# Dividing the softmax at the attention output and exchanging one more unit of the long tiles

## What is computed

```python
x = x + layernorm(attention(layernorm(x)))     # 32 heads of 128 in 8 groups of 4, causal
x = x + layernorm(feed_forward(layernorm(x)))  # 512 -> 1792 -> 512, silu(gate) * up

qkv = q @ w_qkv.T                              # 4096 query, 1024 key, 1024 value columns
scores = einsum('bskgd,btkd->bkgst', qh, kh) / sqrt(128)
scores = where(causal, scores, min_float)
probs = softmax(scores, axis=-1)
attn = einsum('bkgst,btkd->bskgd', probs, vh)
return attn.reshape(...) @ w_dense.T
```

## Time and profile before

| | us |
|---|---|
| median of 3 runs | 1142.49 |
| lowest, highest | 1142.47, 1144.24 |
| span of the profiled execution | 1140.7 |
| TensorE busy in it | 1122.7 |
| VectorE busy | 833.9 |
| ScalarE busy | 626.1 |
| GpSimd busy | 713.9 |

### The profile page before, as it was taken

One profiled execution on the slowest core, in us unless ns is written; L12 is line 12 of the kernel. 1 busy time (PEld: TensorE's weight loads), 2 busy tenths in 40 slices (PEclk: granted clock), 3 DMA queues, 4 the chain that ended last, 5 costly groups with the idle time before them and its releaser, 6 DMA issues.

```text
span 1140.7 us, 17840 instructions
## 1 busy us (share of the span) xinstructions
PE 1122.7 (98%) x5512; PEld 945.5 (83%) x5512; DVE 833.9 (73%) x1987; ACT 626.1 (55%) x1350; POOL 713.9 (63%) x802
## 2 busy tenths in 40 slices
PE   8999999999999999999999999999999989999997
PEld 7888888888888888888888888888887768888885
DVE  5645454557888898888888888988579766666666
ACT  6532324237776767676767767776588532222224
POOL 7844447436674865856757748567784746665645
PEclk9999999999999999999999999999999999999999
DMA  6443555335466475485474665754410033333422
GB/s 224 138 158 148 184 203 185 148 128 183 129 194 218 152 224 183 142 265 173 143 262 127 206 205 159 240 172 121 167 65 1 20 115 114 109 111 92 121 65 98
DMA packets 154696, 173.76 MB, mean 152 GB/s; under 512 B 41776, under 2 KB 128496, under 8 KB 151280
## 3 DMA queue, kind: packets, MB, share of 16 engines
q1 hardware_dynamic: 154608, 172.68, 46.8%
HBM read 101.06 MB, written 71.57 MB: 151 GB/s over the span
## 4 chain that ended last, share of the span: by engine, by line
PE 93%; DVE 2%; POOL 2%; ACT 1%; issue 1%; DMA 0%; POOLq 0%; DVEq 0%; SPq 0%; ACTq 0%
PE psS L1813 29%; PE psOY L1942 17%; PE psOY L1957 15%; PE psOY L1813 15%; PE psT L1813 11%; PE psT L1920 5%; POOL x L1100 0%; DVE pT_lo L1468 0%; PE psS L1819 0%; POOL raw_up L1000 0%; DMA raw<-in_w_v 0%; DVE y L1612 0%; POOL rstd L1031 0%; POOL up_lo L896 0%; DVE probs_long L1533 0%
## 5 line engine op out<-in xcount | busy, mean ns | idle before, releaser
L955 POOL TENSOR_SCALAR probs_long<-probs_long,rsum 128x896 f32<-128x896 f32 (+9 forms) x124 | 129.0, 1042 | 62.3 <-DVE rsum L1539 60.9
L1269 ACT ACTIVATE probs_long<-probs_long,negmax 128x896 f32<-128x896 f32 (+9 forms) x124 | 121.4, 979 | 42.0 <-DVE negmax L1533 39.7
L955 POOL TENSOR_SCALAR probs_short<-probs_short,rsum 128x416 f32<-128x416 f32 (+15 forms) x128 | 69.0, 543 | 120.1 <-DVE rsum L1539 119.7
L1813 PE MATMUL psS<-kT_hi,qT_hi 128*128 128x256 f32 (+8 forms) x384 | 133.0, 346 | 0.0
L1813 PE MATMUL psS<-kT_hi,qT_lo 128*128 128x256 f32 (+8 forms) x384 | 128.3, 334 | 0.0
L1813 PE MATMUL psS<-kT_lo,qT_hi 128*128 128x256 f32 (+8 forms) x384 | 128.1, 334 | 0.0
L1957 PE MATMUL psOY<-wd_hi,oT_hi 128*128 128x512 f32 x256 | 106.8, 417 | 3.3 <-DVE oT_lo L1468 3.3
L1022 POOL TENSOR_SCALAR hidden<-mask,hr,hs 128x128 f32<-128x128 f32 x112 | 50.0, 456 | 86.2 <-DVE hr L1632 82.1
L1957 PE MATMUL psOY<-wd_hi,oT_lo 128*128 128x512 f32 x256 | 101.2, 395 | 0.0
L1957 PE MATMUL psOY<-wd_lo,oT_hi 128*128 128x512 f32 x256 | 100.5, 393 | 0.0
L1264 ACT CAST pT_hi<-square 128x1024 fp32r<-128x1024 f32 (+3 forms) x87 | 77.6, 892 | 31.6 <-DVE square L1552 31.2
(11 more groups left out here) (200 smaller groups left out, 3267.1 us busy)
## 6 DMA issues: line engine op xcount, KB each, us to landing
q_raw<-q_scr SPq DMA_DIRECT2D x64, 256.0 KB, 3.4
p_scr<-probs_long SPq DMA_DIRECT2D x24, 512.0 KB, 3.3
raw<-in_w_qk SPq DMA_DIRECT2D x10, 1024.0 KB, 5.6
p_scr<-probs_long SPq DMA_DIRECT2D x21, 448.0 KB, 2.5
probs_long<-p_scr SPq DMA_DIRECT2D x90, 96.0 KB, 2.8
q_scr<-cB SPq DMA_DIRECT2D x16, 512.0 KB, 2.6
q_scr<-cA SPq DMA_DIRECT2D x16, 512.0 KB, 2.7
raw_wd<-in_w_dense SPq DMA_DIRECT2D x8, 1024.0 KB, 8.4
```

The lines of the kernel that those rows point to most:

```text
L955: nc.gpsimd.tensor_scalar(row, row, rsum[:, column(t, h)], 1.0, ALU.mult, ALU.mult).then_inc(p_ready, 1)
L1269: nc.scalar.activation(row, row, ACT.Exp, bias=negmax[:, column(t, h)], scale=-1.0, accum_out=lsum[:, column(t, h)]).then_inc(e_done, 1)
L1813: last = nc.tensor.matmul(dst, a, b, start=(start and k == 0), stop=(stop and k == len(terms) - 1), skip_group_check=resumed)
```

## The change

1. All 27 exchanged tiles exchange all four units; units 3 and 2 have their low parts on GpSimd, units 1 and 0 on VectorE.

```diff
-    SWAPS = {4: (3, 2, 1), 5: (3, 2, 1), 6: (3, 2, 1), 7: (3, 2, 1, 0)}
-    POOL_LOW = {4: (), 5: (), 6: (), 7: (3,)}
+    SWAPS = {i: (3, 2, 1, 0) for i in range(TPB, NT)}
+    POOL_LOW = {i: (3, 2) for i in range(TPB, NT)}
```

```diff
+            def inverses_away(t):
+                sp.wait_ge(r_done, t + 1)
+                sp.dma_start(r_scr[t % INVERSES], rsum[:, t % INVERSES, :]).then_inc(r_out[t % INVERSES], 16)
+
+            def inverses_back(t):
+                sp.wait_ge(r_out[t % INVERSES], 16 * (t // INVERSES + 1))
+                if t >= 2:
+                    sp.wait_ge(o_scaled, t - 1)
+                sp.dma_start(inverses[t % 2][:], r_scr[t % INVERSES].rearrange("p u -> (p u)").unsqueeze(0).broadcast_to(
+                    [P, BANK])).then_inc(r_in[t % 2], 16)
...
-            def norm_head(t, h):
-                pool.wait_ge(r_done, softmax_count(t, h))
-                row = whole_row(t, h)[:, 0:keys_of(t, h)]
...
-                nc.gpsimd.tensor_scalar(row, row, rsum[:, column(t, h)], 1.0, ALU.mult, ALU.mult).then_inc(p_ready, 1)
+            def zero_tail(t, h):
+                pool.wait_ge(s_done, softmax_count(t, h))
+                nc.gpsimd.memset(probs_long[:, h, S - SPAN * (HG - 1 - h):S], 0.0).then_inc(tail_zero, 1)
+
+            def lo_of_output(t):
+                pool.wait_ge(o_hi, t + 1)
+                low(oT[1][:], o_sb[:], oT[0][:]).then_inc(o_done, 1)
...
-                    act.wait_ge(o_full, args[0] + 1)
-                    nc.scalar.copy(by_head(oT[0]), from_units(psO)).then_inc(o_hi, 1)
+                    act.wait_ge(o_scaled, args[0] + 1)
+                    if args[0] >= 1:
+                        act.wait_ge(y_full, args[0])
+                    nc.scalar.copy(oT[0][:], o_sb[:]).then_inc(o_hi, 1)
...
-            def inverse_sum(t, h):
-                dve.wait_ge(e_done, softmax_count(t, h))
-                nc.vector.reciprocal(rsum[:, column(t, h)], lsum[:, column(t, h)]).then_inc(r_done, 1)
+            def inverse_sums(t):
+                dve.wait_ge(e_done, LAST_SCORE[t] + 1)
+                if t >= INVERSES:
+                    dve.wait_ge(r_out[t % INVERSES], 16 * (t // INVERSES))
+                nc.vector.reciprocal(rsum[:, t % INVERSES, :], lsum[:, t % LANES, :]).then_inc(r_done, 1)
+
+            def scale_output(t):
+                dve.wait_ge(o_full, t + 1)
+                dve.wait_ge(r_in[t % 2], 16 * (t // 2 + 1))
+                if t >= 1:
+                    dve.wait_ge(o_done, t)
+                inverse = inverses[t % 2][:].rearrange("p (b q u) -> p b u q", b=HG, u=HG)
+                nc.vector.tensor_tensor(by_head(o_sb), from_units(psO), inverse, ALU.mult).then_inc(o_scaled, 1)
```

```diff
-                pe.wait_ge(p_ready, softmax_count(t, h))
+                pe.wait_ge(e_done, softmax_count(t, h))
...
-                        pe.wait_ge(o_done, t)
+                        pe.wait_ge(o_scaled, t)
...
+                elif t >= 1 and before_in_row(t) is not None:
+                    k = before_in_row(t)
+                    dve.wait_ge(t_full, TURN["P", k, p_banks(k) - 1, h] + 1)
```

4. New numbers in `PE_LATER`, `ACT_LATER`, `DVE_LATER` and `POOL_LATER` (the `..._MOVES` stay), and SP gets an order of its own for the attention part: a list `LOADS_IN_ORDER` of exchanges, inverses and loads, shifted by `SP_LATER`. Some of it:

```diff
-                ("PV", 0, 0): 2.3, ("X", 0): -37.5, ("DN", 1): -45.7, ("GU", 1): -37.7, ("S", 1, 0): -8.4,
+                ("P", 0, 0, 2): -87.4, ("P", 0, 0, 3): 18.2, ("PV", 0, 0): -12.9, ("PV", 0, 1): -14.8,
...
-            for t in range(2, T):
-                g, n = divmod(t, NT)
-                if t - 3 in SWAPPED:
...
+            for item in moved(LOADS_IN_ORDER, SP_LATER):
+                kind, *args = item
+                if kind == "SA":
+                    swap_away(*args)
```

More of the change, by code:

```diff
@@ L69, in sandwich_kernel @@
     LOADS = 4
+    LANES, INVERSES = 8, 4
     LAG, RING = 4, 4
@@ L271, in in_order @@
                 *ATTENTION[end:]]
+    LOADS_IN_ORDER = []
+    for t in range(2, T):
+        if t - 3 in SWAPPED:
+            away = swaps(t - 3)
+            LOADS_IN_ORDER += [("SA", t - 3, away[0]), *[item for k in range(1, len(away)) for item in (
+                ("SA", t - 3, away[k]), ("SB", t - 3, away[k - 1]))], ("SB", t - 3, away[-1])]
+            LOADS_IN_ORDER += [("RA", t - 3), ("RB", t - 3), ("LQ", t)]
+        else:
+            LOADS_IN_ORDER += [("LQ", t)] + [item for k in {3: (0,), 4: (1,), 2: ()}.get(t, (t - 3,)) for item in (("RA", k), ("RB", k))]
+        if t % NT == 4 and t // NT + 1 < G:
+            LOADS_IN_ORDER += [("LKV", t // NT + 1), ("LD", t // NT + 1)]
+        if t == T - NT + 2:
+            LOADS_IN_ORDER.append(("LC",))
+        if t == T - NT + 3:
+            LOADS_IN_ORDER.append(("LX",))
+    LOADS_IN_ORDER += [(kind, t) for t in range(T - 3, T) for kind in ("RA", "RB")]
     TURN = {item: k for k, item in enumerate(item for item in ATTENTION if item[0] == "P")}
@@ L553, in sandwich_kernel @@
         junk = [at(f"junk{e}", 64 + 2 * e, [P, D]) for e in range(2)]
+        inverses = [at(f"inverses{e}", (132, 146)[e], [P, BANK]) for e in range(2)]
+        o_sb = at("o_sb", 148, [P, BANK])
         oT = [at(f"oT_{p}", 72 + 2 * n, [P, BANK], F32R) for n, p in enumerate(PARTS)]
@@ L586, in sandwich_kernel @@
         s_down_b = small("s_down_b", [P, s_down.shape[1]])
-        negmax, lsum, rsum = (small(n, [P, 2 * HG]) for n in ("negmax", "lsum", "rsum"))
+        negmax = small("negmax", [P, 2 * HG])
+        lsum = small("lsum", [P, LANES, HG])
+        rsum = small("rsum", [P, INVERSES, HG])
         st = small("st", [P, 2, 6])
@@ L692, in whole_row, with row_of, before_in_row, lane @@
             return buffer[:, u, n - (TILES[t] + 1) * P:n]
+        def row_of(t):
+            return "mid" if t == T - 2 else TILES[t] >= TPB
+        def before_in_row(t):
+            return max((k for k in range(t) if row_of(k) == row_of(t)), default=None)
         def column(t, u):
             return slice(SOFT[t, u] % (2 * HG), SOFT[t, u] % (2 * HG) + 1)
+        def lane(t, u):
+            return lsum[:, t % LANES, u:u + 1]
+        def refilled(t, u):
+            return u < HG - 1 and t >= 2 and swapped(t - 2, u) and not swapped(t, u)
+        def refills(t, u):
+            return sum(refilled(k, w) for k, w in SOFT if SOFT[k, w] <= SOFT[t, u])
         def squared(t, u):
@@ L1146, in _ @@
                 nc.gpsimd.memset(probs_short[:, u, BANK - SPAN * (HG - 1 - u):BANK], 0.0).then_inc(const_ready, 1)
-            for h in range(HG):
-                norm_head(0, h)
             pool.wait_ge(p_full, 7 * QUADS)
@@ L1916, in turn_probs @@
                 if b == 0:
-                    pe.wait_ge(p_ready, softmax_count(t, h))
+                    pe.wait_ge(e_done, softmax_count(t, h))
+                    if h == 0 and t < 2:
+                        pe.wait_ge(const_ready, MASKS - (HG - 1) * (1 - t))
+                    if h == 0 and t == T - 2:
+                        pe.wait_ge(const_ready, MASKS + 4 * (HG - 1))
+                    if refilled(t, h):
+                        pe.wait_ge(tail_zero, refills(t, h))
                 bank = psT[:, turn % 2, :]
```

90 lines of the change are left out of this document (49 added, 41 removed), and 400 rows, old and new, of tables (ACT_LATER, DVE_LATER, PE_LATER, POOL_LATER).

## The result

The changed kernel takes 1202.96 us (median of four runs, 1200.59 to 1204.2), the kernel before 1142.56 in runs beside them. The ratio is 1.0523, with a 95% interval of 1.0508 to 1.0538. It is slower by 60 us, where 17 us less were predicted.

What follows compares the result with a forecast made beforehand. TensorE's instructions one after another were taken to bound the kernel. 1140.7 - 13.0 - 6.7 + 1.5 + 1.0 = 1123.5 us for the span, 1125.3 as run median; 80% range 1119.5 to 1136.

Steps and rivals of the forecast that it cites:

- rival D: DMA engines and SP's queue make 27 exchanged tiles wait; 1159 us with the end's holes kept; chance 0.06.
- Part (1): Unit 0 exchanged as well: 126 transposes leave TensorE, 0.9 us of wider scores added, net -13.0 us.
- Part (2): Load on other engines, off the path: VectorE some 60 us, GpSimd 20 to 30 us less busy.
- rival C: GpSimd and VectorE hold each other up at exchanged tiles: 27 x 0.6 = 16 us, 1141 us; chance 0.07.
- Part (3): Softmax divided at the output: multiply 0.68 us, inverses' trip covered; +1.5 us in all groups, +1.0 at the start.
- The "against": Evidence given against rival D: SP's idle time, and peaks of traffic that are short.
- The slack of the exchanged unit: Exchanged unit 0, last score to first value product: path 12 to 14 us, leaving 6 to 9 us of slack.
- Part (4): End of attention: TensorE's waits and slow clock cost 3.0 us instead of 9.7, so -6.7 us.

Runs made afterwards that it cites:

- this last kernel: The changed kernel without the inverses' trip and unit 0's exchange, inverses read in memory order, GpSimd's low parts of exchanged units cut to one block: 1144.7 us.
- late way out: The kernel before with unit 0 exchanged in 21 tiles of index 4 to 6, its way out issued behind the next query load: 1234.1 us.
- padding: The kernel before with one more 256 KB DMA on SP, which nobody waits for, for each of 56 query tiles: 1146.7 us.
- both trips narrow: The changed kernel, inverses' way back cut to 32 columns, unit 0's exchange in 21 new tiles to 128 columns out, 8 a square back: 1164.0 us.

## Why the prediction was wrong

The direction and the mechanism of the loss were rival D's, given 0.06: the DMA engines and SP's queue make exchanged rows late. What D had wrong is what fills them and when.

**Part (1), TensorE's work: right.** 116 transposes are left on the long rows. The matmuls of the two traces, counted by width and priced as in the prediction, make 13.0 us less, as forecast. The saving is real, and every loss measured here is set against it.

**Part (2), the load of the others: off.** GpSimd is 23.2 us less busy, as forecast. VectorE was to be 60 us less busy and is where it was (833.9 before, 833.6). Of the 60 us that VectorE didn't lose, 25 are the multiply, 64 x 0.39. Another 11 are that its 54 low parts of exchanged units take 1257 ns on average, not the 1055 of the earlier trace rows, at the same mean width; the other 24 or so I can't account for. The 768-column ones went from 969 to 1509 ns:

```profile
L1468 DVE TENSOR_TENSOR pT_lo<-square,pT_hi 128x768 fp32r<-128x768 f32 x21 | 20.3, 969 | 3.0 <-ACT pT_hi L1264 2.1
```

```profile
L1620 DVE TENSOR_TENSOR pT_lo<-square,pT_hi 128x768 fp32r<-128x768 f32 x14 | 20.6, 1509 | 0.0
```

With GpSimd's low parts of exchanged units cut, the mean falls from 1390 to 1170, by those of 896 and 640 columns (1491 to 1147, 1295 to 820). Those of 768 columns stay at 1503, because another subtraction of GpSimd, the low part of the dense weight, stands beside them. Two of them and that subtraction in this last kernel:

```profile
467.83 2.92 DVE L1626 TENSOR_TENSOR pT_lo<-square,pT_hi 128x768 fp32r<-128x768 f32 x2
```

```profile
468.00 1.93 POOL L1047 TENSOR_TENSOR wd_lo<-raw_wd,wd_hi 128x512 fp32r<-128x512 f32 x1
```

In the kernel before, two of the one take 1.9 us and the other 1.29. So rival C's hold exists. GpSimd's 54 low parts cost 4.5 us of kernel time, not 16, and what the hold beside the dense weight costs is not measured. The rule behind it in the Trainium skill ("SBUF — State Buffer", "Who interferes with whom") is borne out in direction by these durations; each of the two instructions has two SBUF inputs.

**Part (3), the output path: one price wrong, one step missing.** "Out of PSUM, as the low part, 0.68" took the duration from a row with the same shape and overlooked that one operand is read with a stride: 1.07. It is worth 7 us with free queues, and too little to be seen with full ones. The step that failed is the next: "covered. SP's queue holds loads and exchanges behind them; the awaited events come in order, and SP was idle almost half of the time". The trip itself was covered, as said: TensorE's waits for the multiply and for `oT_lo` are small, the inverses are late for 4.1 us in all. What I didn't ask is what it does to the transfers beside it. It puts two issues and their waits into SP's list and 256 KB, which land after 4.6 us, into the DMA engines for each tile, just where the exchanged rows pass; it is worth 48 us, 49 by the last value product, 30 of them by its width. "Idle almost half of the time" was a misreading of the earlier trace rows: the row is SP waiting, in order, for rows that come in bursts, and what stands behind them can't use that time.

**Rival D: mechanism right, price of the trip wrong.** I gave the pair of transfers 6.2 us and let it decide at 12. The row of the changed kernel shown above took 14.3 us from ready to turned. That of the kernel before with the late way out took 13, of which the landings were 5.9 us, the issues 2.2 and the queue 5.0. The kernel before shows it too, had I looked there: between the end of unit 2's exponential and its transposition lie 10.5 to 12.3 us in its own trace (median 10.8 of 27 tiles), not 6.2. About 1 us of that is GpSimd's multiplication, and as VectorE never waits for a row there, it bounds the trip from above and doesn't measure it. The "against", SP's idle time and short peaks, was the wrong evidence: 0.78 was forecast for the DMA share and 0.80 came, but an average share (0.70 with padding did no harm) doesn't say what waits in line.

**The slack of the exchanged unit: wrong.** "12 to 14 us, from there 6 to 9 us of slack" added a chain of steps as if VectorE were free for each. In the orders of before it isn't, and that costs 1.9 us a tile without any trip; in the changed kernel's own orders it wasn't measured apart.

**Part (4), the end: not had.** TensorE's wait for `oT_lo` between 800 and 960 us went from 3.1 us to 0.5 or 0.7 (1.4 forecast), and in the kernel freed of everything else the clock stays at 1.00. But 9.3 us of holes stand between 800 and 950 us in that kernel, 7.0 stood before between 808 and 935, and 3.0 were forecast. A new wait of 4.8 us, for VectorE's y, took the place of the old ones.

**The sum, from forecast to result**: 1125.3, 19.4 that stay when every known cause is out (to 1144.7), 4.5 for GpSimd's low parts (1149.2), 7.2 the strided operand (1156.4), -1.5 unit 0's trip alone (1154.9), 48.1 the inverses' trip with it there (1203.0), the slower clock included. Except for 1203.0 the measured ones are single runs, so each term may be off by some 2 us. Of the 19.4, the stage table gives some 6 at the end (9.3 where 3.0 were forecast), 2 at the start (3.0 us of holes where 0.2 were and 1.0 more was forecast) and 4 in the steady groups (5.6 us of holes where 0.5 were, and 1.5 forecast). About 7 don't show as idle time; that they are small waits hidden in overlapped records is argued and not shown, and what is the orders' own can't be told apart, since no run has one kernel's orders on the other's work.

## What to carry to other kernels

A transfer with ample time of its own isn't free if it shares an issuing queue with transfers that have none: list what stands in that queue between ready and issued, at the moment of the burst, and price issue time, place and landing, not landing alone; its bytes make every other landing longer as well. Take the length of a round trip from the trace, from the end of the producer to the start of the consumer, rather than by adding two landing times. And when an engine's instruction is priced by another of its shape, compare the strides of all operands first.

## What the runs showed of the hardware

- A DMA issue in a row of issues holds SP for 0.43 us, for 2 KB as for 1 MB, and single ones for longer (0.97 at 451.53 and 1.32 at 454.92 in the changed kernel). Eight ways back in a row took 3.8 us at best in both kernels, 4.4 by the median before and 4.5 after, and 5.17 in the stretch shown above; the fuller DMA engines of the changed kernel don't lengthen the issues.

```profile
451.06 5.17 SPq L870 DMA_DIRECT2D probs_long<-p_scr  x8
```

- At a DMA share of 0.80 the way out of 512 KB lands after 4.3 to 4.6 us, 3.1 at 0.60. The share alone doesn't set it: 4.0 us at 0.64 with both trips narrow, 3.3 at 0.69 without the inverses' trip.
- A VectorE multiply of 128x512 with PSUM and SBUF operands takes 1070 ns with a stride of 16 bytes in SBUF, 681 without.
- 2 KB written in words of 4 bytes land after 10.5 us instead of 3.3, and transfers beside them land up to twice as late (9.3 for 4.7 us).
- GpSimd spends 0.6 us on a DMA issue, ScalarE 0.33 on its queue, beside its own instructions.
- TensorE's granted clock fell to its lower level behind a hole of 4.33 us: products of 448 columns started 0.37 us apart instead of 0.20.
- A VectorE and a GpSimd subtraction with two SBUF inputs each lengthen one another: two of 768 columns took 2.92 us instead of 1.9, the one of 512 columns beside them 1.93 instead of 1.29.
